# Last expert stage: gate and up weights split into halves per tile by ScalarE and VectorE, products in three single passes

## The reference

```python
logits = h2 @ router_w
probs = jax.nn.softmax(logits, axis=-1)
topw, topi = jax.lax.top_k(probs, TOP_K)
topw = jax.nn.softmax(topw, axis=-1)
combine = jnp.sum(jax.nn.one_hot(topi, N_EXPERTS, dtype=h2.dtype) * topw[..., None], axis=1)
shared = swiglu(h2, sh_gate, sh_up, sh_down)
gate = jnp.einsum('td,edf->etf', h2, e_gate)
up = jnp.einsum('td,edf->etf', h2, e_up)
eout = jnp.einsum('etf,efd->etd', jax.nn.silu(gate) * up, e_down)
spec = jnp.einsum('etd,te->td', eout, combine)
```

## Time and profile before

| what | us |
|---|---|
| median of 3 runs | 2359.95 |
| lowest and highest of them | 2357.28 to 2373.63 |
| the profiled execution | 2357.93 |
| its span, first to last instruction | 2356.2 |
| its mean granted TensorE clock, as a share of the full one | 0.917 |

### The profile page before, as it was taken

One profiled execution on the slowest core, in us unless ns is written; L12 is line 12 of the kernel. 1 busy time (PEld: TensorE's weight loads), 2 busy tenths in 40 slices (PEclk: granted clock), 3 DMA queues, 4 the chain that ended last, 5 costly groups with the idle time before them and its releaser, 6 DMA issues. The chain is left out here.

```text
span 2356.2 us, 39785 instructions
## 1 busy us (share of the span) xinstructions
PE 2013.2 (85%) x15304; PEld 1466.6 (62%) x15304; DVE 1041.3 (44%) x2771; ACT 849.0 (36%) x2148; POOL 649.7 (28%) x609
## 2 busy tenths in 40 slices
PE   5888957998389999379999995998599996999995
PEld 4677745664368888257777774665466665666663
DVE  2666654565323232235555554555355653312222
ACT  3655532342123232325555543432233332222222
POOL 1433334662422322223333332111100000412222
PEclk9999987997589999689999998997699997999998
DMA  2000011000523422510000002000400003722223
GB/s 59 11 10 20 15 39 32 10 24 15 187 87 106 143 73 44 183 38 2 11 19 10 10 6 63 10 24 15 133 15 15 28 14 127 279 57 46 46 46 91
DMA packets 100034, 127.49 MB, mean 54 GB/s; under 512 B 8682, under 2 KB 86970, under 8 KB 99818
## 3 DMA queue, kind: packets, MB, share of 16 engines
q1 hardware_dynamic: 86554, 107.17, 13.9%
q0 software_dynamic: 13296, 17.77, 4.4%
HBM read 87.12 MB, written 39.89 MB: 54 GB/s over the span
## 5 line engine op out<-in xcount | busy, mean ns | idle before, releaser
L2035 POOL TENSOR_TENSOR L1a_probs<-L1a_probs,L1a_rinv 128x1024 f32<-128x1024 f32 x64 | 121.2, 1894 | 286.3 <-DVE L1a_rinv L2357 286.3
L2032 POOL TENSOR_TENSOR L0a_probs<-L0a_probs,L0a_rinv 128x256 f32<-128x256 f32 (+1 forms) x128 | 103.1, 826 | 203.5 <-DVE L0a_rinv L2357 203.4
L2349 DVE CUSTOM_DVE_ANT_0 L1a_sbias<-L1a_psS,L1a_bias 128x256 f32<-128x256 f32 x256 | 93.2, 421 | 123.7 <-PE L1a_psS L2166 123.7
L2280 ACT ACTIVATE L1a_probs<-L1a_sbias,L1a_nmx 128x256 f32<-128x256 f32 x256 | 126.5, 498 | 40.0 <-DVE L1a_nmx L2349 40.0
L2783 DVE TENSOR_TENSOR ec_hT<-ec_sg,ec_psU 128x512 f32<-128x512 f32 x64 | 44.0, 688 | 194.5 <-ACT ec_sg L2713 194.5
L3228 DVE TENSOR_TENSOR moe_h<-moe_h,moe_psU 128x512 f32<-128x512 f32 x55 | 37.8, 687 | 194.8 <-PE moe_psU L3047 194.8
L2280 ACT ACTIVATE L0a_probs<-L0a_sbias,L0a_nmx 128x128 f32<-128x128 f32 (+1 forms) x256 | 112.8, 443 | 29.8 <-DVE L0a_nmx L2349 29.8
L2654 PE MATMUL ec_psA<-ec_wd,ec_hT 128*128 128x256 f32 x512 | 112.6, 381 | 5.2 <-DVE ec_hT L2783 5.2
L2998 POOL DMA_INDIRECT moe_sums<-moe_y,moe_xg x39 | 60.8, 1559 | 201.1 <-DVE moe_y L3240 198.1
L2589 POOL DMA_INDIRECT ec_sums<-ec_yk,ec_token_at x32 | 50.4, 1574 | 228.7 <-ACT ec_yk L2721 223.8
L2654 PEld LDWEIGHTS ec_psA<-ec_wd,ec_hT 128*128 128x128 f32 x512 | 96.6, 190 | 20.1 <-DVE ec_hT L2783 7.3
(11 more groups left out here) (486 smaller groups left out, 4725.2 us busy)
## 6 DMA issues: line engine op xcount, KB each, us to landing
ec_wg<-in_L_ffn_w_gate SPq DMA_DIRECT2D x8, 1024.0 KB, 8.7
ec_wu<-in_L_ffn_w_up SPq DMA_DIRECT2D x8, 1024.0 KB, 12.3
ec_wd<-in_L_ffn_w_down SPq DMA_DIRECT2D x8, 1024.0 KB, 5.8
moe_rows<-blank SPq DMA_DIRECT2D x1, 5070.0 KB, 21.2
moe_xg<-moe_rows SPq DMA_DIRECT2D x39, 130.0 KB, 2.1
moe_wts<-in_L_ffn_e_gate SPq DMA_DIRECT2D x8, 512.0 KB
moe_wts<-in_L_ffn_e_up SPq DMA_DIRECT2D x8, 512.0 KB
moe_wts<-in_L_ffn_e_down SPq DMA_DIRECT2D x8, 512.0 KB
```

What stands on the lines that cost most here:

```text
L2032: last = pool.tensor_tensor(v, v, bcast(rinv[:, r, :, t], 2, KEYS[t]), ALU.mult)
L2035: last = pool.tensor_tensor(v, v, bcast(rinv[:, r, :, :].rearrange("p h t -> p (h t)"), 2, S), ALU.mult)
L2280: ins = act.activation(probs[:, r, j, at], sbias[:, g % 2, j, at], ACT.Exp, bias=nmx[:, r, j, t:t + 1], scale=-1.0, accum_out=sums[:, r, j ...
L2349: last = dve.tensor_tensor_reduce(out=sbias[:, g % 2, j, at], in0=psS[:, slot + j, at], in1=added, scale=-1.0, scalar=LARGE, op0=ALU.add, ...
```

## The change

Gate and up are computed from halves. `x` and the weights are each split into a high part (a copy to fp32r by ScalarE) and the rest (what the copy left out, by VectorE), and each fp32 product becomes three fp32r products: high with high, high with rest, rest with high.

- The weights of a tile are split two tiles ahead: `high_expert(n)` and `rest_expert(n, j, e)` make the halves of routed tile n (from 1) while tile g = n + 13 is worked on, into one of two buffers `wt`. A register, loaded by ScalarE and VectorE for each tile, gives the expert's place in `wts`. This is done for every tile, whether or not its expert is that of the tile before. The shared expert's weights are split once (`high_shared`, `rest_shared`).
- The second buffer lies in the memory of `xT`, so its first use waits until the last shared tile's x is split.
- x of a tile is split one tile ahead (`high_x`, `rest_x`), from `xT` for a shared tile, from `psX` for a routed one; `gT` and `take_rows` are gone. The next turning of rows waits for the rest.
- `h` has one buffer instead of two. Silu of g waits until h of g - 1 is turned.
- Down still reads `wts` by a register, in fp32. The rows of routed tile 0 are now turned during the last shared tile.

```diff
--- before.py
+++ after.py
...
-        xT = sb("xT", [P, NT, KD, P])
+        with nc.sbuf_tensor("moe_xT", [P, NT, KD, P], F32) as xT:
+            pass
+        wt_in_xT = sb("wt_in_xT", [P, 2, 2, KD * F], F32R)
+        wt = [sb("wt", [P, 2, 2, KD * F], F32R), wt_in_xT]
...
-        gT = sb("gT", [P, 2, KD, P])
-        h = sb("h", [P, 2, F])
+        xs = sb("xs", [P, 2, 2, KD * P], F32R)
+        h = sb("h", [P, F])
...
@@ -3034,31 +3038,36 @@
                 def turn_rows(j):
                     pe.wait_ge(xg_loaded[j % RX], 16 * (j // RX + 1))
                     if j:
-                        pe.wait_ge(gT_ready, j)
+                        pe.wait_ge(x_rest, NT + j)
...
-                def up(g, e, x):
+                def up(g):
                     if g >= 2:
                         pe.wait_ge(h_ready, g - 1)
+                    pe.wait_ge(x_rest, g + 1)
+                    n = max(g - NT + 1, 0)
                     for j, ps, done in ((0, psG, gate_ready), (1, psU, up_ready)):
+                        pe.wait_ge(w_rest[j], n + 1)
                         for c in range(KD):
-                            last = pe.matmul(ps[:, g % 2, :], x[:, c, :], weights(e, j)[:, c * F:(c + 1) * F],
-                                             start=(c == 0), stop=(c == KD - 1))
+                            for k, (a, b) in enumerate(((0, 0), (0, 1), (1, 0))):
+                                last = pe.matmul(ps[:, g % 2, :], xs[:, g % 2, a, c * P:(c + 1) * P],
+                                                 wt[n % 2][:, b, j, c * F:(c + 1) * F],
+                                                 start=(c + k == 0), stop=(c == KD - 1 and k == 2))
                         last.then_inc(done, 1)
 
...
-                pe.wait_ge(shared_loaded, 48)
-                for t in range(NT):
-                    if t:
-                        turn_h(t - 1)
-                    up(t, E, xT[:, t, :, :])
-                    if t == 1:
+                before = E
+                for g in range(NG):
+                    if g:
+                        turn_h(g - 1)
+                    if NT <= g + 1 < NG:
+                        turn_rows(g + 1 - NT)
+                    up(g)
+                    if g == 1:
                         ranks()
-                    if t:
-                        down(t - 1, E)
-                pe.wait_ge(owner_ready, 1)
-                turn_h(NT - 1)
-                turn_rows(0)
-                e, before = pe.value_load(owner_at[0:1, 0:1], min_val=0, max_val=E - 1), E
-                pe.wait_ge(experts_loaded, 48 * E)
-                for j in range(NR):
-                    g = NT + j
-                    if j:
-                        turn_h(g - 1)
-                    if j + 1 < NR:
-                        turn_rows(j + 1)
-                    pe.wait_ge(gT_ready, j + 1)
-                    up(g, e, gT[:, j % 2, :, :])
-                    down(g - 1, before)
-                    before = e
-                    if j + 1 < NR:
-                        e = pe.value_load(owner_at[0:1, j + 1:j + 2], min_val=0, max_val=E - 1)
+                    if g == NT:
+                        pe.wait_ge(experts_loaded, 48 * E)
+                    if g:
+                        down(g - 1, before)
+                    if g >= NT - 1 and g + 1 < NG:
+                        if g == NT - 1:
+                            pe.wait_ge(owner_ready, 1)
+                        before = E if g == NT - 1 else e
+                        e = pe.value_load(owner_at[0:1, g + 1 - NT:g + 2 - NT], min_val=0, max_val=E - 1)
+                    elif g + 1 == NG:
+                        before = e
                 turn_h(NG - 1)
                 down(NG - 1, before)
...
@@ -3112,14 +3115,11 @@
...
                 def silu(g):
                     act.wait_ge(gate_ready, g + 1)
-                    if g >= 2:
-                        act.wait_ge(h_turned, g - 1)
-                    act.activation(h[:, g % 2, :], psG[:, g % 2, :], ACT.Silu).then_inc(silu_ready, 1)
+                    if g:
+                        act.wait_ge(h_turned, g)
+                    act.activation(h[:], psG[:, g % 2, :], ACT.Silu).then_inc(silu_ready, 1)
...
-                def take_rows(j):
-                    act.wait_ge(xg_turned, j + 1)
-                    if j >= 2:
-                        act.wait_ge(up_ready, NT + j - 1)
-                    act.activation(gT[:, j % 2, :, :].rearrange("p c s -> p (c s)"), psX[:, 0:D], ACT.Copy)\
-                        .then_inc(gT_ready, 1)
...
-                for t in range(NT):
-                    if t:
-                        take_h(t - 1)
-                    silu(t)
-                take_h(NT - 1)
-                take_rows(0)
-                for j in range(NR):
-                    if j:
-                        take_h(NT + j - 1)
-                    if j + 1 < NR:
-                        take_rows(j + 1)
-                    silu(NT + j)
+                def high_x(g):
+
+                    if g >= 2:
+                        act.wait_ge(up_ready, g - 1)
+                    if g < NT:
+                        src = xT[:, g, :, :].rearrange("p c s -> p (c s)")
+                    else:
+                        act.wait_ge(xg_turned, g - NT + 1)
+                        src = psX[:, 0:D]
+                    act.activation(xs[:, g % 2, 0, :], src, ACT.Copy).then_inc(x_high, 1)
+
+                def high_shared():
+                    act.wait_ge(shared_loaded, 48)
+                    for j in range(2):
+                        act.activation(wt[0][:, 0, j, :], wts[:, E, j, :], ACT.Copy).then_inc(w_high[j], 1)
+
+                def high_expert(n):
+
+                    if n == 1:
+                        act.wait_ge(x_rest, NT)
+                        act.wait_ge(owner_ready, 1)
+                        act.wait_ge(experts_loaded, 48 * E)
+                    else:
+                        act.wait_ge(up_ready, NT + n - 2)
+                    e = act.value_load(owner_at[0:1, n - 1:n], min_val=0, max_val=E - 1)
+                    for j in range(2):
+                        act.activation(wt[n % 2][:, 0, j, :], wts[:, bass.ds(e, 1), j, :].rearrange("p o f -> p (o f)"), ACT.Copy)\
+                            .then_inc(w_high[j], 1)
+
+                high_shared()
+                high_x(0)
+                act.wait_ge(shifted, 1)
+                act.activation(pr[:], pr[:], ACT.Exp).then_inc(exps, 1)
+                for g in range(NG):
+                    if g:
+                        take_h(g - 1)
+                    if g + 1 < NG:
+                        high_x(g + 1)
+                    silu(g)
+                    if 1 <= g - NT + 3 <= NR:
+                        high_expert(g - NT + 3)
                 take_h(NG - 1)
...
@@ -3225,7 +3247,23 @@
                 def product(g):
                     dve.wait_ge(silu_ready, g + 1)
                     dve.wait_ge(up_ready, g + 1)
-                    dve.tensor_tensor(h[:, g % 2, :], h[:, g % 2, :], psU[:, g % 2, :], ALU.mult).then_inc(h_ready, 1)
+                    dve.tensor_tensor(h[:], h[:], psU[:, g % 2, :], ALU.mult).then_inc(h_ready, 1)
+
+                def rest_x(g):
+                    dve.wait_ge(x_high, g + 1)
+                    src = xT[:, g, :, :].rearrange("p c s -> p (c s)") if g < NT else psX[:, 0:D]
+                    dve.tensor_tensor(xs[:, g % 2, 1, :], src, xs[:, g % 2, 0, :], ALU.subtract).then_inc(x_rest, 1)
+
+                def rest_shared():
+                    for j in range(2):
+                        dve.wait_ge(w_high[j], 1)
+                        dve.tensor_tensor(wt[0][:, 1, j, :], wts[:, E, j, :], wt[0][:, 0, j, :], ALU.subtract)\
+                            .then_inc(w_rest[j], 1)
+
+                def rest_expert(n, j, e):
+                    dve.wait_ge(w_high[j], n + 1)
+                    dve.tensor_tensor(wt[n % 2][:, 1, j, :], wts[:, bass.ds(e, 1), j, :].rearrange("p o f -> p (o f)"),
+                                      wt[n % 2][:, 0, j, :], ALU.subtract).then_inc(w_rest[j], 1)
...
@@ -3240,27 +3278,41 @@
...
+                rest_shared()
+                rest_x(0)
                 probabilities()
                 choose(0, pr)
+                rest_x(1)
                 product(0)
                 choose(1, rest)
                 gap()
+                rest_x(2)
                 product(1)
                 counts()
                 take_shared(0)
+                rest_x(3)
                 product(2)
                 combine()
                 places()
                 take_shared(1)
+                rest_x(4)
                 product(3)
                 owners()
                 take_shared(2)
                 for g in range(4, NG):
+                    n = g - NT + 3
+                    if g + 1 < NG:
+                        rest_x(g + 1)
                     product(g)
+                    if 1 <= n <= NR:
```

(4 more changed lines are left out.)

15 lines of the change are left out of this document (7 added, 8 removed).

## The result

The changed kernel takes 2330.55 us (median of 4 runs, 2325.83 to 2336.28), the kernel before beside it 2364.95 us (4 runs, 2357.28 to 2373.63): a ratio of 0.9855, 95% interval 0.9808 to 0.9901. The forecast was 2320 us, range 2308 to 2344. So the time fell by 34 us where 39 had been worked out, and 5 us of the distance to 2320 is that the kernel before came out at 2364.95 here and not at 2359.95. The profiled execution took 2332.3 us, with a span of 2330.6.

The account below looks back on a forecast made before the run. TensorE's own work bounds the last stage; start 0.4, shared tiles 10.1 and routed stretch 28.9 us, less 0.2 for the scatter, save 39.2 us: 2318.7 from the profiled 2357.93, forecast as 2320 us, range 2308 to 2344.

Parts of the forecast that it names:

- rival 2: Routed tiles: the splitting engines set the pace, VectorE's cycle 5.4 us, 2332 us in all; chance 0.11.
- The bound: Last stage: TensorE's own work is the bound, busy 195.00 of 195.00 us, with no gap in a routed tile.
- The price of a product: Gate and up on TensorE: 12 single-pass products at 0.227 us, 2.72 us instead of 3.44, saving 0.72 us a tile.
- The sum's 39 x 5.10 + 0.22: Routed stretch to the last turning of h: 199.1 us against 228.0, so 28.9 us saved.
- What it adds on ScalarE and VectorE: Routed tiles: ScalarE 4.2 us and VectorE 4.1 to 4.6 us of work, under the 5.10 us period, costing TensorE nothing.
- The forecast's clock of the steps: Timetable of a routed tile at period 5.10 us: next VectorE product 0.05 us late, cover 0.7 us on VectorE.
- rival 3: Routed tiles: GpSimd's transfers hold VectorE's subtractions, VectorE's cycle 6.4 us, 2371 us in all; chance 0.04.
- The scatter: GpSimd's chained adds of y: 4.60 us start to start, held by VectorE's subtractions, yet fit 5.10 us by 0.5.
- rival 1: TensorE's single-pass product is cheaper, 0.215 us, saving 8 us more, 2312 us in all; chance 0.12.
- The start: Start of the last stage: first gate 1.7 us late for the splits, second turning of h still 0.4 us earlier.
- slow pace: First gate of the last stage: 3.71 us instead of 1.88; lasting over the whole first tile, 1 us worse.
- Rival 5: Gate and up: each product still costs its four passes, so the change does not do what it says; chance 0.01.

Follow-up runs that it names:

- Run 11: Changed kernel plus 416 bytes of padding ahead of moe_xs and ScalarE's shared-weight copies before its last two x copies: 2325.71 us, ratio 0.9828.
- run 8: Changed kernel with only moe_xs moved in SBUF, allocated ahead of all other tensors: 4.92 us a shared tile, 5.14 us a routed tile.
- run 10: Changed kernel with 32 bytes per partition of padding ahead of moe_xs: 4.96 us a shared tile, 5.16 us a routed tile.
- kind 3 of run 2: Changed kernel, but every fourth shared tile loads its held operand from the split weights instead of the rows, weights still streamed: 4.92 us a tile.
- kinds 1 and 2 of run 9: Changed kernel, some shared tiles loading and streaming one tensor: split weights 4.93 us a tile, split rows 4.91 to 4.92 us.
- run 1: Changed kernel without weight splitting and its register loads from the third routed tile on: 5.18 us a routed tile, 2330.48 us in all.
- run 3: Changed kernel with two more unused VectorE subtractions of 128x512 in each routed tile: 5.30 us a routed tile in the mean.
- run 4: Changed kernel with VectorE taking y ahead of both weight subtractions instead of between them: 5.18 us a routed tile.
- run 6: Changed kernel with ScalarE copying the shared weights ahead of its last two copies of x: 2332.09 us, ratio 0.9858.
- run 5: Changed kernel with the shared tiles' gate and up products done once, twice or three times in a row: 4.97, 7.78 and 10.59 us a tile.

## Why the prediction was right, and where it was short

The account below rests on the periods, not on the total. By the total alone, 2330.55 us stands nearer to rival 2's 2332 than to the forecast's 2320, and that is chance: rival 2 wanted a routed tile of 5.4 us with TensorE waiting for VectorE, and measured are 5.18 us without a wait. And the forecast had no term for the clock ahead of the stage, which moved its start by 25 us between profiles; that the time fell within 2308 to 2344 is in part luck.

**The bound.** TensorE set the pace before and does so after; 155.00 of 155.00 us busy. Right.

**The price of a product** is the step that failed in size: "I take 12 x 0.227 = 2.72 us for one tile". Net the dozen cost 2.80 us. Over the 53 periods between the second and the last turning of h that is 0.08 x 53 = 4.2 us, all that the two large stretches came out short. (The sum's 39 x 5.10 + 0.22 also counts forty turnings of rows where there are 39, 0.2 us too much; the shared tiles' 0.09 us makes up for it.) The clean comparison is between like with like. The earlier trace rows are sound, but they stand in the middle of a run of 96 products. Such runs stand in the kernel before eight times; the seven that follow down products have, behind a first record of 0.42 us, two to nine records of 0.224 to 0.236 us, and only then stay at 0.227. Ours have a first record of 0.317, and after it never leave 0.228 to 0.238.

The first record looks dearer than it is. It starts 0.03 us behind the start of the last record ahead of it, where one of that kind otherwise takes 0.11 us (turnings) or 0.22 (down, ahead of the run of 96). With that taken off, the first product costs 0.24 and 0.23 us, like those behind it. So there is no large price for entering such a run; all of its first products cost a little more.

Run 11 parts the 0.09 us that a shared tile came out over its forecast: 0.05 is that the products don't settle in their place in SBUF (4.97 against 4.92), and 0.04 is the stretch before they do (4.92 against 4.88). In the routed tiles the three other places took off 0.04 (run 8), 0.02 (run 10) and 0.01 us (run 11). Which rule of addresses stands behind this is open: start addresses equal modulo 512 went with settling wherever they held, sooner or later in the dozen (the earlier stage, where ec_xs lies right behind the 32 KB of ec_wt, kind 3 of run 2, kinds 1 and 2 of run 9, run 11), yet run 8, where they are not equal, has the shortest routed tile. Why a run starts unsteady is open too.

The page "TensorE: Matmul & The Clock Gate" of the Trainium skill, section "Wait — 56ns, not 53.3ns?", puts a product at 0.216 us; the runs show a steady 0.227 at best. By that page, an estimate, the forecast would have erred by 7 us more.

**What it adds on ScalarE and VectorE.** Hidden, as worked out (run 1). The sizes were near: 2.01 us for ScalarE's two copies against 2.1, 1.22 for a subtraction against 1.22. The register loads took 0.28 and 0.30 us (medians in ns below), some 0.5 with their arithmetic, as taken from TensorE's:

```profile
L3154 ACTq TENSOR_LOAD <-moe_owner_at x39: 273/276/478, 2090.9 to 2289.1; - x39
```

```profile
L3308 DVEq TENSOR_LOAD <-moe_owner_at x39: 299/302/554, 2092.3 to 2289.2; - x39
```

The forecast's clock of the steps was too tight by about half a microsecond (run 3). With that rivals 2 and 3 fall: TensorE has no wait for VectorE in the routed tiles, it is GpSimd that is stretched, and no subtraction took more than 1.23 us.

**The scatter.** Right, in the mechanism too: the adds grow (to 2.20 us), stand still until the subtraction is over, and fit. The margin given was 5.10 - 4.60 = 0.5 us; measured it is 5.18 - 4.5 = 0.7 (run 4 and the rows at 2123.95 to 2137.54). With products at 0.215 us (rival 1) the period would have been 4.96 us, still above 4.5, so the adds should have kept up; no run shows that. The shortest period that they were seen to keep is run 8's 5.14.

The Trainium skill, "SBUF — State Buffer", practical consequences, has a VectorE instruction with two SBUF inputs contend with a GpSimd instruction that reads SBUF. The runs agree for GpSimd: 2.20 us with the subtractions, 1.56 without (run 1).

**The start.** Forecast 0.4 us gained, measured none. The first gate came 1.3 us later behind the start of the stage than before (21.25 against 19.96 us), where 1.7 was forecast. But from there to the second turning of h it took 11.6 us, not 10.7. The "slow pace" that the prediction feared is the granted clock, 0.50 until about 4.0 us behind the gate's start, against 3.6 before (estimates from its means over four microseconds). The wait ahead of the gate was 1.15 us by its row; without it the start is 1.0 to 1.8 us shorter (runs 6 and 11).

**The border.** The stall of 1 us between shared and routed tiles went as forecast; no wait stands at 2098.95.

**Rival 5** is excluded by the periods and by six records for each of gate and up.

## What to carry to other kernels

Read the price of an instruction from a stretch like the one it will stand in: as many in a row, after the same kind of work, and from the first to what follows the last. A steady value from the middle of a long run is the lower end of the range, not its middle. And when work is moved to idle engines, see what else reads memory beside it, and compare the hold-up with the slack of what is held: here the splitting stretched GpSimd's adds from 1.56 to 2.20 us, but their chain needs 4.5 us and had 5.18.

## What was not expected of the hardware

Single-pass products of 512 columns at full clock settle at 0.227 us or never do, by where their two operands lie in SBUF: 0.234 us each throughout a run of 36 (run 5). Padding of 416 bytes took 0.05 us off every shared tile, and the move of one 4 KB tensor 0.05 us off every shared and 0.04 us off every routed one. Adds that wait for one another start 4.3 to 4.6 us apart when nothing holds them, and an add that meets a subtraction of VectorE ends 3.04 us behind the start of its y wherever between 0.75 and 1.43 us it starts. With both subtractions behind the take of y a late add is held by the second and does not catch up (run 4).
